# Cross-attention and quantised FFN on one core: softmax denominators moved from TensorE to VectorE

## What is computed

```
q  = layernorm(layernorm(x)) @ Wq            # x: 8 x 1024 x 512
k, v = split(layernorm(ctx) @ Wkv)           # ctx: 8 x 64 x 512, 16 heads of 64
attn = softmax(clip(q k^T / 8, -11, 11))     # over the 64 context rows
x1 = x + (attn v) @ Wo + bo
xq = fake_quant(layernorm(x1))               # one scale for the tensor
h  = fake_quant(silu(xq @ Wg^T) * (xq @ Wu^T))
out = x1 + h @ Wd^T
```

## Time and profile before

| | before |
|---|---|
| median of 3 runs | 1309.81 us (1308.99 to 1311.67) |
| span of the profiled execution | 1307.3 us |
| TensorE busy | 1273.7 us (97%) |
| VectorE busy | 1147.7 us (88%) |
| ScalarE busy | 805.3 us (62%) |
| GpSimd busy | 302.5 us (23%) |
| granted TensorE clock | 1.00 |

### The profile page before, as it was taken

The page is one execution under the profiler, slowest core; times in us unless marked ns, Lnnn a source line. Parts: engine busy times, 40 slices in busy tenths (PEclk is TensorE's granted clock), DMA queues, the critical chain, the costliest instruction groups (busy, mean ns, idle before and its releaser), DMA issues.

```text
span 1307.3 us, 20769 instructions
## 1 busy us (share of the span) xinstructions
PE 1273.7 (97%) x7756; PEld 605.4 (46%) x7800; DVE 1147.7 (88%) x2086; ACT 805.3 (62%) x1211; POOL 302.5 (23%) x230
## 2 busy tenths in 40 slices
PE   6999999999999999999999999999999999989998
PEld 4644444544445445445445444444444444434443
DVE  7777988898998889899888848799999999889998
ACT  6589577567557757755775762233333333399993
POOL 3105242244134224413422420000000000013223
PEclk9999999999999999999999999999999999999999
DMA  7276057247146355462562392196667642389997
GB/s 298 78 238 186 22 150 223 68 129 202 65 142 181 106 163 120 125 206 57 159 227 73 106 240 87 45 306 229 198 259 249 217 173 85 113 306 420 421 420 305
DMA packets 182437, 241.76 MB, mean 185 GB/s; under 512 B 122032, under 2 KB 141248, under 8 KB 169920
## 3 DMA queue, kind: packets, MB, share of 16 engines
q1 hardware_dynamic: 182336, 240.43, 55.6%
HBM read 120.86 MB, written 90.57 MB: 162 GB/s over the span
## 4 chain that ended last, share of the span: by engine, by line
PE 65%; DVE 13%; ACT 12%; DMA 4%; issue 3%; SPq 1%; POOL 1%; DVEq 0%; ACTq 0%
PE pg L1584 10%; PE pu L1590 10%; PE po L77 7%; PE po L79 7%; PE po L78 7%; PE ring L79 6%; PE ring L77 6%; PE ring L78 6%; ACT hb L1448 6%; DMA out_dram<-xqT 1%; ACT E L452 1%; DMA x<-in_x_dram 1%; PE ring L1039 1%; PE ring L1066 1%; ACT E L446 1%
## 5 line engine op out<-in xcount | busy, mean ns | idle before, releaser
L1426 ACT ACTIVATE sg<-pg,gate_scale 128x512 f32<-128x512 f32 x176 | 121.0, 687 | 184.0 <-PE pg L1584 184.0
L77 PE MATMUL ring<-yT,M 128*128 128x512 f16 x512 | 194.1, 379 | 0.0
L79 PE MATMUL ring<-yT,M 128*128 128x512 f16 x512 | 194.0, 379 | 0.0
L78 PE MATMUL ring<-yT,M 128*128 128x512 f16 x512 | 194.0, 379 | 0.0
L77 PE MATMUL po<-VW,p 128*128 128x512 f16 x480 | 182.2, 380 | 1.7 <-DVE p L660 1.7
L79 PE MATMUL po<-VW,p 128*128 128x512 f16 x480 | 181.9, 379 | 0.0
L78 PE MATMUL po<-VW,p 128*128 128x512 f16 x480 | 181.9, 379 | 0.0
L1584 PE MATMUL pg<-xqT,w 128*128 128x512 bf16 x690 | 178.8, 379 | 2.2 <-ACT xqT L1437 0.8
L1590 PE MATMUL pu<-xqT,w 128*128 128x512 bf16 x689 | 178.6, 379 | 0.8
L395 POOL TENSOR_TENSOR esum<-esum,E 128x512 f32<-128x512 f32 x96 | 130.5, 1359 | 83.8 <-ACT E L456 83.8
L467 ACT ACTIVATE p<-E 128x512 f16<-128x512 f32 x120 | 74.9, 625 | 121.6 <-DVE E L656 119.6
(11 more groups left out here) (246 smaller groups left out, 2060.0 us busy)
## 6 DMA issues: line engine op xcount, KB each, us to landing
hidden<-hb SPq DMA_DIRECT2D x11, 2816.0 KB, 9.9
xa<-x_rows_d SPq DMA_DIRECT2D x28, 1024.0 KB, 5.6
hb<-hidden SPq DMA_DIRECT2D x22, 1024.0 KB, 16.4
x<-in_x_dram SPq DMA_DIRECT2D x16, 1024.0 KB, 5.7
value_fold<-E SPq DMA_DIRECT2D x64, 256.0 KB, 2.5
VW<-value_fold SPq DMA_DIRECT2D x16, 1024.0 KB, 6.0
x_rows_d<-x SPq DMA_DIRECT2D x16, 1024.0 KB, 4.6
out_dram<-xa SPq DMA_DIRECT2D x11, 1024.0 KB, 13.3
```

The costliest lines, as they stand in the source:

```text
L77: nc.tensor.matmul(out, a_hi, b_hi, start=first, stop=False)
L78: nc.tensor.matmul(out, a_hi, b_lo, start=False, stop=False)
L79: return nc.tensor.matmul(out, a_lo, b_hi, start=False, stop=last)
L1426: nc.scalar.activation(sg[:, n % 4], pg[n % 4][:], ACT.Silu, scale=gate_scale[:, n % FT:n % FT + 1]).then_inc(silus, 1)
```

## The change

TensorE no longer takes part in the denominators. VectorE does all of it within `invert`: it transposes `esum` (128x512) in blocks of 32x32, so that tokens stand on partitions and a block's four heads and eight slots along the free dimension (`esum_by_token`); adds up the 8 slots (128x64); inverts; and transposes back, each value read 8 times in a row, straight into PSUM `pd`. `divide` becomes a `scalar_tensor_tensor`, which also multiplies by PROB_GAIN, since `head_cols` is gone. GpSimd's next group of sums now waits for the first transpose in place of the TensorE product. Three GpSimd instructions, one TensorE and one VectorE instruction that built `head_cols` at the start go too.

```diff
@@ sums on GpSimd
             if t == 1:
-                wait(pool, dens, g)
+                wait(pool, sums_turned, g)
                 nc.gpsimd.tensor_tensor(esum[:], E[:, g % 2, 0], E[:, g % 2, 1], ALU.add).then_inc(sums, 1)
@@ invert on VectorE
         def invert(g):
+
+            dve.wait_ge(sums, 7 * g + 7)
+            nc.vector.transpose(esumT[:].rearrange("p n s -> p (n s)"), esum[:]).then_inc(sums_turned, 1)
+            dve.wait_ge(sums_turned, g + 1)
+            nc.vector.tensor_reduce(dsum[:], esumT[:], AX.X, ALU.add).then_inc(dens, 1)
             dve.wait_ge(dens, g + 1)
-            nc.vector.reciprocal(rtok[:].rearrange("p t h -> p (t h)"), pd[:, 0:TT * H]).then_inc(rdens, 1)
-            dve.wait_ge(rdens, 2 * g + 1)
-            nc.vector.tensor_copy(rexp[:], rtok[:].rearrange("p t (h a) -> p t h a", a=1).broadcast_to((P, TT, H, KS))).then_inc(rdens, 1)
+            nc.vector.reciprocal(rsum[:], dsum[:]).then_inc(rdens, 1)
+            dve.wait_ge(rdens, g + 1)
+            wait(dve, prob, 8 * g)
+            nc.vector.transpose(pd[:].rearrange("p (n s) -> p n s", s=KS),
+                                rsum[:].rearrange("p (n a) -> p n a", a=1).broadcast_to((P, GT // KS, KS))).then_inc(rden_turned, 1)
 
         def divide(g, t):
             if t == 0:
                 dve.wait_ge(rden_turned, g + 1)
             dve.wait_ge(exps, 8 * g + t + 1)
-            nc.vector.tensor_tensor(E[:, g % 2, t], E[:, g % 2, t], pd[:], ALU.mult).then_inc(prob, 1)
+            nc.vector.scalar_tensor_tensor(E[:, g % 2, t], E[:, g % 2, t], PROB_GAIN, pd[:], ALU.mult, ALU.mult).then_inc(prob, 1)
@@ TensorE
-        def denominators(g):
-            pe.wait_ge(sums, 7 * g + 7)
-            wait(pe, prob, 8 * g)
-            for t in range(TT):
-                ins = nc.tensor.matmul(pd[:, t * H:(t + 1) * H], esum[:, t * P:(t + 1) * P], keep.head_cols[:], start=True, stop=True)
-            ins.then_inc(dens, 1)
-
-        def turn_back(g):
-            pe.wait_ge(rdens, 2 * g + 2)
-            for t in range(TT):
-                ins = nc.tensor.transpose(pd[:, t * P:(t + 1) * P], rexp[:, t].rearrange("p h s -> p (h s)"), keep.ident32[:])
-            ins.then_inc(rden_turned, 1)
```

More of the change, by code:

```diff
@@ L112, in attention @@
     esum = sb("esum", [P, GT], fp32)
-    rtok = sb("rtok", [P, TT, H], fp32)
-    rexp = sb("rexp", [P, TT, H, KS], fp32)
+    esumT = sb("esum_by_token", [P, GT // KS, KS], fp32)
+    dsum = sb("den_by_token", [P, GT // KS], fp32)
+    rsum = sb("rden_by_token", [P, GT // KS], fp32)
     stage = E[:, 1].rearrange("p t n -> p (t n)").bitcast(fp16).rearrange("p (k a q n) -> p k a q n", k=4, a=2, q=2)
@@ L181, in attention @@
     scores, capped, floored, exps, sums = sem("scores"), sem("capped"), sem("floored"), sem("exps"), sem("sums")
-    dens, rdens, rden_turned = sem("dens"), sem("rdens"), sem("rden_turned")
+    sums_turned, dens, rdens, rden_turned = sem("sums_turned"), sem("dens"), sem("rdens"), sem("rden_turned")
     prob, prob_hi, prob_lo = sem("prob"), sem("prob_hi"), sem("prob_lo")
@@ L375, in on_gpsimd @@
                                    base=0, pattern=[[-1, P]], channel_multiplier=1))
[L376 to L380, removed]
         nc.gpsimd.memset(magic[:, 0:1], MAGIC).then_inc(magic_set, 1)
@@ L769, in vectors_seen @@
             nc.vector.tensor_scalar(row_reach, keep.ident32[0:4 * DC, 0:4 * DC], amax[0:4 * DC, 0:1], None, ALU.mult).then_inc(spread_in, 1)
-            dve.wait_ge(const_turned, 2)
-            do(nc.vector.tensor_scalar(keep.head_cols[:], misc[:, 4 * DC:4 * DC + H], 1.0 / PROB_GAIN, None, ALU.mult))
+            dve.wait_ge(const_turned, 1)
             do(nc.vector.tensor_copy(cols[:].rearrange("p k c -> p (k c)"), misc[:, 0:4 * DC]))
@@ L1077, in fold, with output @@
                 fold_values(values_folded_in(s), u // 2)
-        def output(g, t, between):
+        def output(g, t):
             if t == 0:
@@ L1090, in output @@
                                      k == 0, k == KT - 1)
-                if k == 1 and t in (1, 2):
-                    between(t - 1)
             ins.then_inc(outs, 1)
@@ L1136, in product @@
             if n == 0:
-                pe.wait_ge(made, 5 + 2 * DC)
+                pe.wait_ge(made, 2 + 2 * DC)
                 pe.wait_ge(w_lo[1], DC)
@@ L1169, in turn_q @@
             ins.then_inc(q_turned, 1)
-        pe.wait_ge(made, 5)
-        nc.tensor.transpose(misc[:, 4 * DC:4 * DC + H], keep.head_rows[:], keep.ident32[0:H, 0:H]).then_inc(const_turned, 1)
+        pe.wait_ge(made, 2)
         pe.wait_ge(ld_vec, 64)
@@ L1219, in on_tensor @@
                     fold_values(0, t // 2)
[L1220 to L1229, removed]
             for t in range(TT):
                 if s > 0:
-                    output(s - 1, t, between)
+                    output(s - 1, t)
                     for u in FOLD_AFTER[t]:
@@ L1237, in on_tensor @@
         for t in range(TT):
-            output(NG - 1, t, lambda k: None)
+            output(NG - 1, t)
     return on_sync, on_gpsimd, on_scalar, on_vector, on_tensor
@@ L1646, in program @@
         keep.ident32 = sb("ident32", [P, P], fp32)
-        keep.head_cols = sb("head_cols", [P, H], fp32)
-        keep.head_rows = sb("head_rows", [H, P], fp32)
         keep.own_row = sb("own_row", [P, KS], fp32)
```

## The result

The changed kernel takes 1328.62 us (median of 4 runs, 1328.02 to 1329.0) against 1309.78 (4 runs, 1308.99 to 1311.67) beside it: 1.0142 times as long, 95% interval 1.013 to 1.0154, **18.84 us more**. The forecast was 17.5 more.

What follows compares the result with a forecast made beforehand. A ScalarE-VectorE loop nearly as long as TensorE's step passes on VectorE's added work: 14 x 1.72 = 24.1, less 1.7, 2.4 and 2.5, gives +17.5 us, 1327.3 us; range 1317 to 1343.

Steps and rivals of the forecast that it cites:

- The loop beside TensorE: Steps 2 to 14: ScalarE's 21 us and VectorE's 24 us, waiting in turn, match TensorE's 45.84 us step within 1.7 in 12 steps.
- VectorE's piece from the last `low_y` to the second `divide`: Sign in steps 2 to 14: this stretch of VectorE's work, with `invert` in it, gets 1.7 us longer.
- The 4.6 us of idle: VectorE's idle in each of steps 2 to 13, taken as waiting for ScalarE, so unable to absorb the added work.
- VectorE added, 1.72 us a group: In `invert`: transpose, sum of slots, reciprocal and transpose back take 2.65 us instead of 0.93, so 1.72 more per group.
- Less the 1.7 us of waiting for TensorE: Groups 0 to 13: 24.1 us of loop delay first eats 1.7 us of VectorE's waits for TensorE, leaving 22.4.
- 2.4 us kept: Output part of step 14: the last `low` ends 2.4 us before the first output tile's eighth slice, so 2.4 us come off.
- 1.24 saved in the output parts of steps 14 and 15: TensorE is last there again, so its removed products and transposes save 1.24 us for each of two groups, 2.5 us.
- group 15's `invert` hidden under the 7.92 us: Step 15: VectorE waits 7.92 us for output tiles, so that group's added 1.72 us was to cost nothing.
- Rival A: Whole kernel: the loop gives way, TensorE stays the bound, and its saved 19.8 us come off, 1290.0 us; chance 0.08.
- Rival B: VectorE's transposes in `invert` take two passes, 1.21 us each, 2.76 more a group: +32.0 us, 1341.8; chance 0.14.
- Rival C: Whole kernel about equal, 1310 us, if both engines' margins happen to cancel; chance 0.05.
- Rival D: TensorE's granted clock falls from 1.00 as its loop waits grow to some 3 us a step; time well above Rival B's; chance 0.03.

Runs made afterwards that it cites:

- the third run: Changed kernel with TensorE's eight small instructions per group put back at their old places, on constants into an unread PSUM bank: 1330.46 us, ratio 1.0156.

## Why the prediction was right, and where it was off

The time, the sign and the mechanism were right; the forecast of 1327.3 was 1.3 us short. Step by step:

- **The loop beside TensorE** (first part of the prediction): shown, by the three runs that relieve, load and load back. Of its signs, the `take`'s wait for TensorE is gone, ScalarE's busy stretch is unchanged, `low` releases TensorE, and the wait of a group's first `high` grew, from 6.3 to 9.4 us in step 5, by more than the 1.7 that were forecast. VectorE's piece from the last `low_y` to the second `divide` grew by 1.31 us in step 5 (23.61 to 24.92), less than the 1.7 of that sign, mostly because its wait of 0.34 for TensorE has gone from it. `invert` doesn't wait for GpSimd in the steps. The 4.6 us of idle that the forecast saw in each VectorE step don't count `low` held up beside GpSimd, which the profile shows as busy (last section).
- **VectorE added, 1.72 us a group**: 1.74. The terms: transposes 0.69 each, measured 0.70 and 0.73; sum of slots 0.69, measured 0.69; reciprocal 0.55, measured 0.55; the edges of 0.04 and 0.09 held. The estimate from the Trainium skill (VectorE: DVE Perf Modes, The three transpose paths), 0.71 us, holds as well; the two are too close for the run to part them. The same page's rule (Rules for kernel authors), TensorE where a transpose may end in PSUM, would have been right for this kernel as it was ordered, and wrong for it once ScalarE's order was changed.
- **Less the 1.7 us of waiting for TensorE**: too small. This step took the loop's slack from the waits that VectorE's `take` shows, 1.3 + 0.4 us. The step with TensorE relieved is 45.54 us against 45.84: 0.30 us a step, some 3.6 over twelve. The reciprocal of group 13 shows the same: it came 20.7 us later than before (715.49 against 694.76), of which 1.45 are the transpose and the sum ahead of it, so 19.3 for 13 groups; 13 x 1.74 would be 22.6, and 3.3 went into slack. A visible wait at one instruction is only what is left of an engine's slack after its neighbours have taken theirs. Steps came to 47.30 us, not 47.4.
- **2.4 us kept (2.47 by the rows), then 1.24 saved in the output parts of steps 14 and 15**: the first held (the loop's 19.3 and group 13's 1.74, less 1.24, less the 17.7 found at step 15, leave 2.1), the second only in step 14. Forecast were 20.0 us of delay ahead of them, 18.8 by step 15 and 17.5 by the FFN. Measured: 17.7 by step 15, as the larger slack of the loop would have it, and then *plus* 1.17 in place of minus 1.24. The step that failed is the sentence that called group 15's `invert` hidden under the 7.92 us: it stands behind that `take` in VectorE's order, not ahead of it, so the wait can't hide it. In the changed kernel VectorE then has no gap from 799.95 until the last `low`, and TensorE waits 2.42 us for it, where the kernel before had 1.86, at full clock. The 2.41 us between minus 1.24 and plus 1.17 have two halves. At full clock, in the run with two caps ahead, the part from step 15's output to the FFN takes 56.73 us against 56.81 before, so the late `invert` eats 1.16 of the 1.24. The other 1.25 (57.98 against 56.73, the same waits) went with the half clock, for which the sum had no term. Two errors of about 1.1 and 2.4 us on opposite sides make the 1.3 that the forecast was short; that it came so close is partly luck.
- **Not seen at all**: TensorE's wait of 1 us before each fourth output tile, for the second `take`, which VectorE reaches later. It cost nothing, since the loop was the bound; the products given back in the third run fill it.
- **Rival A**, 1290.0, was refused for ScalarE's order, and this was its true condition: with `cap` ahead of the second `high` and the other highs behind by one tile the time is 1295.0, and 1292.9 with the last `invert` moved. The 2.9 us that are still missing lie ahead of step 2. From there to the FFN that last version takes 656.23 us against 673.84 before, 17.6 less, and 14 groups of 1.24 are 17.4. But step 2 starts 0.64 us later (160.38 against 159.74), where two groups' 1.24 would have it 2.5 earlier: in step 1 TensorE waits 2.25 and 2.27 us for `low` and falls to half clock.
- **Rival B** is out by the transposes' 0.70 and 0.73 us. **Rival C** is out with them.
- **Rival D** came true in small. It was put at waits of some 3 us a step; the clock fell behind single waits of 2.3 and 2.4, in two places of a few microseconds, and cost some 1.25 us in the second. As a mechanism for the whole time it was not there: 1.00 over steps 2 to 13.

## What to carry to other kernels

Before work is moved off the busiest engine, look for a ring of waits among the others that is nearly as long as that engine's step, and measure it by relieving the engine with nothing added; the visible waits understate its slack (1.7 us here for 3.3). If the work would land in the ring, cut the ring first: here a few lines moved in the order of ScalarE and VectorE turned 18.8 us of loss into 15 of gain. And whether a wait hides an instruction is decided by which of the two stands first in the engine's order.

## What the runs showed of the hardware that was not expected

- **Granted clock.** In the kernel before it is 1.00 in both of these places. With the change it fell to half, from 2.4 to 1.2 GHz, in step 1 behind two waits of TensorE of 2.24 and 2.27 us (0.61 us a matmul at 137.27) and in step 15 behind one of 2.42 (0.64 at 823.82). The length of the wait doesn't decide it. In step 15 the clock stayed at 1.00 behind 2.42 us in the run with two caps ahead, shown above. It stayed there behind 1.86 us in the kernel before, in the one with the same order, in the one with VectorE loaded and in the one with the last `invert` moved. It fell behind 1.86 us in the one with TensorE relieved and in the one with its load given back:

```profile
823.80 0.39 PE L77 MATMUL po<-VW,yT 128*128 128x512 f16 x1 [1.86 <-DVE yT L663]
...
825.00 0.61 PE L77 MATMUL po<-VW,yT 128*128 128x512 f16 x1 [0.38 <-DVE yT L663]
```

  What decides stays open. What it costs can be read where TensorE's instructions and longest wait are alike and the clock is not, from step 15's output part to the FFN: 57.98 (the change), 57.28 and 57.21 (the highs one tile later, twice) against 56.73, and 56.84 (TensorE relieved) against 55.56. That is 0.5 to 1.3 us each time, enough to blur a difference of a microsecond between two executions.
- **VectorE beside GpSimd.** In step 5 of the kernel before `low` takes 0.69 us at 302.83, with no GpSimd instruction under way. This one stands beside a sum of GpSimd's that runs for 1.27 us from 309.06:

```profile
309.11 1.76 DVE L660 TENSOR_TENSOR p<-E,p 128x512 f16<-128x512 f32 x1
```

  It ends 0.54 us behind that sum. Over the twelve steps 60 of the 96 start while GpSimd is at work; each of them takes 1.27 to 1.77 us and ends 0.53 to 0.56 us behind GpSimd's instruction, and the other 36 take 0.68 to 0.69. So VectorE's busy share holds time in which it is held up. With the new order `low` starts later and its mean over the whole kernel falls from 1.17 to 0.85 us. No run shows what that is worth in time.
- **VectorE's transpose of 4-byte data** takes 703 ns for 128x512 in blocks, 727 with a source read eight times in a row and PSUM as its end: close to the sum of slots and the `divide` over 512 columns here (686 and 674 ns), though not to the copy's 0.43 us. The Trainium skill's table (VectorE: DVE Perf Modes, The three transpose paths) names SBUF alone as where it goes; this trace shows PSUM too. Followed by an instruction that doesn't depend on it, it held the engine for 0.62 us.
